# 28 keep-busy matmuls around the first weight spread, 14 on each side, in place of 10 behind it

## The reference, cut to what matters

```python
# x is (32, 64, 56, 56) float32; w1, w2 are (64, 64, 3, 3)
def quantize_weight(w, bits):                 # bits = 8
    scale = jnp.max(jnp.abs(w)) / (2.0 ** (bits - 1) - 1.0)
    return jnp.round(w / scale) * scale

def layer(x):                                 # conv3x3 has padding 1
    out = conv3x3(x, quantize_weight(w1), b1)
    out = relu(batchnorm(out, gamma1, beta1)) # mean and variance over images, rows, columns
    out = batchnorm(conv3x3(out, quantize_weight(w2), b2), gamma2, beta2)
    return relu(out + x)

def gn(v, G=32): ...                          # each image, groups of two channels: mean 0, variance 1

x = x + layer(gn(x))
```

## Time and profile before

| | |
|---|---|
| median of three runs | 548.16 us |
| the profiled execution: its time | 548.97 us |
| its span, first to last instruction | 547.2 us |
| TensorE busy | 395.0 us (72%) |
| VectorE busy | 463.2 us (85%) |
| ScalarE busy | 329.5 us (60%) |
| mean granted TensorE clock | 0.879 of full |

### The profile page before, as it was taken

The page is one execution under the profiler, slowest core; times in us unless marked ns, Lnnn a source line. Parts: engine busy times, 40 slices in busy tenths (PEclk is TensorE's granted clock), DMA queues, the critical chain, the costliest instruction groups (busy, mean ns, idle before and its releaser), DMA issues.

```text
span 547.2 us, 20478 instructions
## 1 busy us (share of the span) xinstructions
PE 395.0 (72%) x9497; PEld 342.6 (63%) x9497; DVE 463.2 (85%) x590; ACT 329.5 (60%) x350; POOL 91.6 (17%) x147
## 2 busy tenths in 40 slices
PE   2998989999999999999999999999990000000000
PEld 1786979999998887898888998888880000000000
DVE  7986999999999955997888897788868999999960
ACT  2787769999998963766555556655506826443100
POOL 2025386566662500000000000000000000000000
PEclk9999999999999999999999999999996555555555
DMA  8999000045433000034443300000066988999998
GB/s 299 421 425 407 20 7 8 9 144 208 148 133 124 8 12 7 2 133 167 153 156 124 122 4 4 4 2 4 2 238 222 365 334 310 431 425 432 432 426 380
DMA packets 16349, 99.21 MB, mean 181 GB/s; under 512 B 5896, under 2 KB 7560, under 8 KB 9352
## 3 DMA queue, kind: packets, MB, share of 16 engines
q1 hardware_dynamic: 14640, 81.55, 37.9%
q10 hardware_dynamic: 1624, 16.36, 7.5%
HBM read 61.48 MB, written 35.50 MB: 177 GB/s over the span
## 4 chain that ended last, share of the span: by engine, by line
PE 66%; DVE 16%; issue 9%; ACT 3%; POOL 1%; DMA 1%; SPq 0%; DVEq 0%; ACTq 0%
PE conv_ps L959 64%; DVE slots L914 10%; DVE slots L917 2%; DVE gn_tup L650 1%; DMA slots<-in_x_dram 1%; PE conv_ps L923 1%; DVE xa L917 1%; POOL gn_tmp L375 1%; ACT split L424 1%; ACT split L416 1%; ACT slots L453 1%; DVE conv_ps L914 1%; DVE slots L704 0%; DVE split L717 0%; POOL gn_tmp L372 0%
## 5 line engine op out<-in xcount | busy, mean ns | idle before, releaser
L959 PE MATMUL conv_ps<-split,wmat 64*64 64x385 f16 (+3 forms) x9144 | 380.1, 325 | 5.5 <-issue 3.3
L959 PEld LDWEIGHTS conv_ps<-split,wmat 64*64 64x64 bf16 x9144 | 331.0, 107 | 50.9 <-issue 7.5
L453 ACT ACTIVATE slots<-conv_ps,par,evac_scale 128x784 f32<-128x784 f32 x124 | 124.0, 1001 | 100.6 <-PE conv_ps L959 98.8
L750 DVE BATCH_NORM_STATS2 bn_tup<-slots 128x6 f32<-128x392 f32 x164 | 81.0, 556 | 16.0 <-ACT slots L453 16.0
L576 ACT ACTIVATE slots<-slots,skip_b,bn_w 128x3136 f32<-128x3136 f32 (+3 forms) x20 | 46.0, 2345 | 43.8 <-DVE slots L917 24.8
L717 DVE TENSOR_TENSOR split<-slots,split 128x3136 f16<-128x3136 f32 (+4 forms) x32 | 57.0, 1791 | 7.9 <-ACT slots L432 5.1
L650 DVE BATCH_NORM_STATS2 gn_tup<-slots 128x6 f32<-128x448 f32 x112 | 61.5, 611 | 2.1 <-DMA slots<-in_x_dram 2.1
L719 DVE SCALAR_TENSOR_TENSOR split<-slots,split 128x3248 f16<-128x3248 f32 (+3 forms) x18 | 53.6, 2979 | 2.6 <-DVE slots L704 0.5
L704 DVE TENSOR_SCALAR slots<-slots,bn_w 128x3248 f32<-128x3248 f32 (+3 forms) x18 | 30.4, 1687 | 21.6 <-ACT split L416 20.9
L416 ACT ACTIVATE split<-slots,bn_w 128x3248 f16<-128x3248 f32 x14 | 43.2, 3085 | 0.0
L461 ACT ACTIVATE xa<-conv_ps,par,evac_scale 128x784 bf16<-128x784 f32 x41 | 40.9, 1001 | 0.0
(11 more groups left out here) (121 smaller groups left out, 214.3 us busy)
## 6 DMA issues: line engine op xcount, KB each, us to landing
slots<-in_x_dram SPq DMA_DIRECT2D x16, 1568.0 KB, 22.8
out_dram<-slots SPq DMA_DIRECT2D x13, 1568.0 KB, 27.0
split<-in_x_dram ACTq DMA_DIRECT2D x5, 1568.0 KB, 17.1
y_spill<-slots SPq DMA_DIRECT2D x3, 1624.0 KB, 7.3
slots<-y_spill SPq DMA_DIRECT2D x3, 1624.0 KB, 6.9
y_spill<-slots SPq DMA_DIRECT2D x3, 1568.0 KB, 5.8
xa<-in_x_dram ACTq DMA_DIRECT2D x3, 1568.0 KB, 17.8
slots<-y_spill SPq DMA_DIRECT2D x3, 1568.0 KB, 28.6
```

Of the source, the lines that this page charges most:

```text
L453: nc.scalar.activation(dst, src, ACT.Identity, bias=bias, scale=scale, accum_out=total).then_inc(evacuated[ph], 1)
L750: ins = nc.vector.bn_stats(bn_tup[:, 2 * (n - first) + s, :], rows[s])
L959: return nc.tensor.matmul(bank[:, r0:r1, w0:w1], lhs, rows[:, top + r0:top + r1, w0 + kx - 1:w1 + kx - 1], start=n == 0 and part is hi_all ...
```

## The change

The ten keep-busy matmuls behind the spread become fourteen, and fourteen more are put ahead of the spread's wait, behind the two waits for identities and constants. No wait, semaphore or DMA is added or moved. Both blocks use the zeroed `wmat[1]`.

```diff
             pe.wait_ge(ident_made, 1)
             pe.wait_ge(consts_set, 7)
+            keep_warm(1, 14)
             spread_absmax(0)
-            keep_warm(1, 10)
+            keep_warm(1, 14)
             weight_transposes(0)
             keep_warm(1, 2)
             pe.wait_ge(params_loaded, 6 * 16)
```

## The result

The changed kernel is slower. Its median is 550.07 us over 18 runs (548.91 to 551.09), against 548.57 us for the kernel before over 18 runs (547.71 to 549.77). The ratio is 1.0025, 95% interval 1.0018 to 1.0032: 1.4 us more, where 0.65 us less was forecast. The profiled execution took 549.83 us, its span 548.0.

The account below looks back on a forecast made before the run. TensorE was taken as the bound, with instruction supply behind the loads of x at least as slow from 24.6 to 55.4 us. Blocks 0, clock -1.3, supply +0.65 gave -0.65: 548.16 to 547.5 us, range 546.7 to 548.9.

Parts of the forecast that it names:

- Front and back block at no cost on the path: Keep-busy blocks around the spread: front ends near 8.3 us, before the spread at 9.07; back before transposes at 14.0; cost 0.
- The clock is up ahead of the first convolution: Start of TensorE's work: the added keep-busy matmuls bring 2.4 GHz before the first convolution, where before it rose about 18.3 us.
- Does it last over the 2.0 us of idle? ... It lasts: Idle between back block and transposes: the full clock holds, since it held from 410.6 to 413.0 at the end of phase 1.
- Clock, -1.3 us: First convolution round at full clock ends at 18.9 us instead of 20.2, a gain of 1.3 us.
- Supply, +0.65 us: Instruction blocks before 55 us: 36 more instructions put boundaries 0.74 us earlier in the work, taking back 0.65 us.
- "slower" rival: Clock gains nothing and supply takes its toll at boundaries up to 55 us; 549.0 to 549.2 us, chance 0.1.
- Behind 79.81 TensorE runs with no long break: Long stretch after 79.81 us: TensorE has no long break and the rest of the kernel hangs on it in order.
- crossing a block is mostly hidden: Skill's rule on instruction fetch at 256-instruction boundaries; basis of the rival that supply doesn't bind, 546.9 to 547.0 us, chance 0.2.
- the rival without gain: Clock falls again before the convolutions or rises as late as before; time 548.2 us, chance 0.2.

Follow-up runs that it names:

- e5: Kernel before with the front block alone: 14 keep-busy matmuls ahead of the spread, 10 behind as before; 549.41 us, ratio 1.0014.
- e11: Changed kernel with loads of x from the sixth pair on issued a quarter at a time, one after each evacuated round; 547.30 us, ratio 0.9976.
- e3: Changed kernel with only the first five loads of x issued at once, each later one when a pair is convolved; 547.32 us, ratio 0.9985.
- e1: Kernel before plus 18 small 2-column matmuls (36 instructions) in TensorE's first idle time; 549.58 us, ratio 1.0020.
- e4: Changed kernel with 27 keep-busy matmuls behind the spread in place of 14; 548.61 us, ratio 0.9998 against the kernel before.
- e9: Changed kernel with 27 keep-busy matmuls behind the spread and loads of x spread out, five at once, later ones per convolved pair; 546.25 us, ratio 0.9957.
- e12: Changed kernel with 27 keep-busy matmuls behind the spread and quarter loads of x after each evacuated round; 546.43 us, ratio 0.9964.
- e14: Changed kernel run again with the same code, for a second profile; 549.55 us, ratio 1.0024 against the kernel before.
- e2: Kernel before with only the first five loads of x issued at once, each later one when a pair is convolved; 549.00 us, ratio 1.0017.
- e15: Kernel before run again with the same code, a single run for a second sample of its clock; 549.47 us.
- e10: Kernel before with loads of x from the sixth pair on issued a quarter at a time, one after each evacuated round; 545.72 us, ratio 0.9959.

## Why the prediction was wrong, point by point

*Front and back block at no cost on the path:* right. The spread went at 9.03, the transposes at 13.90.

*The clock is up ahead of the first convolution:* right as far as it goes. With fourteen matmuls ahead it rose between 6.49 and 8.43 us in seven of eight executions, and in e5 at 13.06.

*"Does it last over the 2.0 us of idle? ... It lasts":* wrong, and the first step that failed. The clock fell at 13.93 in the profiled execution, at 14.88 in the second and at 15.25 in e11; in e3 alone, of four executions of this prologue, it didn't. My evidence was one stretch in which the clock held, and it was itself the beginning of a fall. What it showed was that one idle time of 2.4 us had been survived, not that 2.2 us always are. Nor does the length of the idle time decide alone: e1 had 1.30 us and a fall, e3 2.17 us and none. In the executions without idle time (e4, e9, e12) there was no fall.

*Clock, -1.3 us:* wrong at both ends. The changed kernel gained 0.54 us at the first round, and 0.43 in e14, where it was taken at 19.81. And the late rise of the profiled execution of before isn't the rule: in four executions of its prologue (before, e2, e15, e10) the clock rose at 18.35, 18.27, 13.31 and 12.60. I carried the profile's clock over to the median all the same.

*Supply, +0.65 us:* right in kind, too small in size, and applied to the wrong gain. In the profiled execution boundaries stand nearly still while the work is 0.74 us behind at each. The second boundary fell at 29.54, an interval of 6.2 us (the upper end that I named), an advance of 0.50 on 30.04. Less 0.74 that is a loss of 0.24 us there, and 0.42 by round (2, 1); with the 0.54 gained before, supply took 0.96 us. This is my "slower" rival, with its rule (a loss if the advance is under 0.74 us) met; I gave it 0.1 because I asked for the clock's gain to be absent altogether, and half a gain was small enough. In e14 it went the other way: the second boundary came at 28.64 without a stop, an interval of 5.3 us, and round (2, 1) was taken at 49.43, 0.81 us before that of before. So whether an early gain came was a matter of the execution; the stop near 140 us came in both.

*"Behind 79.81 TensorE runs with no long break":* wrong. I had tied stops to the loads of x before 55 us and didn't follow DMA's share to 138 us. That missed 0.52 us, over a third of the cost, and it is the one part that every trace of these ends shows.

*The account:* in the profiled pair, 0.42 up to 80 us and 0.52 at 141 us make 0.94, and 0.86 is what the spans differ by. The medians differ by 1.4 to 1.5. Executions in which before starts with the clock up don't explain the rest: the one in e15 was worth nothing by 80 us. The profiled executions of before lie 0.4 and 1.0 us over their medians, those of the changed kernel and of e1 0.2 to 0.6 under, so the traces show less of the difference than the medians. About 0.9 us of the 1.4 is not located. Of the distance to the forecast, 0.4 us is its base: before measured 548.57 over 18 runs, where the three I had gave 548.16.

*The skill's rules:* that crossing a block is mostly hidden ("Runtime: NRT & Kernel Launch" of the Trainium skill, Instruction fetch mechanics) doesn't hold where a load of x or a spill is under way: stops of 0.4 to 1.1 us. That transposes don't count as busy for the clock ("TensorE: Matmul & The Clock Gate" of the Trainium skill, Part 4) was my reason for the rival without gain. The runs don't show it: the clock fell just as the transposes began in the profiled execution (13.93 against 13.90), but 1.0 us after they had ended in e14, and the idle time stands ahead of them each time.

What stays open: the shares of clock and supply in the 1.4 us. The 36 instructions cost 1.1 by themselves (e1), and e4, which holds the clock, gives back 1.4, but moves the ends too; the two overlap, since a block that is asked for late or early moves every stop behind it.

## What to carry to other kernels

In a fully unrolled kernel TensorE's instruction stream is a transfer like any other, and behind large loads it can be the bound: look for "issue" stops with 127 or 128 matmul pairs between them, through the whole span. Before adding warm-up matmuls, count their instructions and see where the ends of the blocks move; a gain ahead of a stop that DMA sets is lost at it. Breaking up the loads, so that an instruction packet never queues behind 1.6 MB, was worth more here (0.9959) than any warm-up by itself (at best 0.9998). Before trusting an account made from one profile, take a second one of each kernel: here the two of one kernel differ by 1.3 us at 79 us. And a warm-up that ends 2 us before the work may leave the clock halved for just that work.

## What the runs showed of the hardware that I hadn't expected

- The same code gets its clock at different times: 18.35 and 13.31 us in two executions of the kernel before, 7.10 and 8.06 in two of the changed one, 6.49 in the changed prologue with other loads.
- From the start of an instruction packet to TensorE's next weight load it took 2.2 to 2.6 us at the late ends, loads under way or not (33.77 to 36.22 before, 138.80 to 141.15 after, 137.14 to 139.32 in e11); what varied was how long the packet waited to start.
- An end of a block may have hardly any slack without a sign of it in the profile: the one at 140.87 before became a stop of 0.49 to 0.61 us in six traces in which it lies 0.74 us earlier in the work.
